# A four-layer conditional residual block: the transpose of the normalised rows moved from TensorE to VectorE

## The reference, cut to what matters

```
x = x + L0(x)    # adapter: relu(x @ W1 + b1) @ W2 + b2, plus x, layer norm over the row, * gamma + beta
x = x + L1(x)    # x @ weight[subject].T + bias
x = x + L2(x)    # two experts and three shared networks, relu(x @ wi) @ wo, mixed by a gate
x = x + L3(x)    # scores by tanh(x @ W1 + b1) @ v, masked softmax over rows, pooled rows
```

## Time and profile before

| | |
|---|---|
| median of 3 runs | 500.68 us (500.46 to 500.73) |
| the profiled execution | 501.22 us |
| its span, first to last instruction | 499.4 us |
| TensorE matmuls | 99% of the span busy |
| VectorE | 70% |
| ScalarE | 52% |
| GpSimd | 47% |

### The profile page before, as it was taken

How to read it: one execution, slowest core, us unless ns; L and a number is a source line. 1 busy time by engine, 2 the same in 40 slices (tenths; PEclk the granted TensorE clock), 3 DMA queues, 4 the chain that set the end, 5 groups by cost and what they waited for, 6 DMA issues and landing times.

```text
span 499.4 us, 6992 instructions
## 1 busy us (share of the span) xinstructions
PE 493.0 (99%) x2320; PEld 407.7 (82%) x2320; DVE 348.8 (70%) x702; ACT 260.3 (52%) x506; POOL 236.0 (47%) x201
## 2 busy tenths in 40 slices
PE   8999999999999999999999999999999999999996
PEld 5787888888888888888888888888888888888985
DVE  5587235885688799786478689788568779644467
ACT  4655555543457574444446656454345757445243
POOL 1575446445264446444544447444525444746023
PEclk9999999999999999999999999999999999999999
DMA  5865354322255443422227454422222342331002
GB/s 154 185 185 150 101 147 147 100 85 85 85 120 145 116 115 87 127 85 84 85 85 169 123 161 123 132 84 85 85 85 85 100 112 84 88 131 37 0 1 84
DMA packets 77657, 52.97 MB, mean 106 GB/s; under 512 B 40758, under 2 KB 67382, under 8 KB 77622
## 3 DMA queue, kind: packets, MB, share of 16 engines
q1 hardware_dynamic: 75734, 50.44, 35.5%
q10 hardware_dynamic: 1888, 2.10, 1.3%
HBM read 48.33 MB, written 2.10 MB: 101 GB/s over the span
## 4 chain that ended last, share of the span: by engine, by line
PE 90%; DVE 5%; DMA 3%; issue 1%; ACT 0%; ACTq 0%; DVEq 0%; SPq 0%
PE ps_hid L839 14%; PE ps_hid L840 14%; PE ps_hid L844 14%; PE ps_net L901 13%; PE ps_net L896 13%; PE ps_net L897 13%; DMA raw_wo<-in_L_cond_share_wo_dram 3%; PE ps_net L868 2%; DVE pick L1680 1%; DVE hid_lo L1827 1%; PE ps_side L537 1%; PE ps_side L541 1%; PE ps_side L536 1%; PE ps_side L547 1%; PE ps_side L550 1%
## 5 line engine op out<-in xcount | busy, mean ns | idle before, releaser
L1924 POOL TENSOR_TENSOR wi_lo<-raw_wi,wi_hi 128x512 fp32r<-128x512 f32 x77 | 101.6, 1319 | 207.5 <-ACT wo_hi L1088 110.2
L1109 ACT ACTIVATE hid_hi<-ps_hid 128x512 fp32r<-128x512 f32 x160 | 95.5, 598 | 194.1 <-PE ps_hid L844 192.3
L1827 DVE SCALAR_TENSOR_TENSOR hid_lo<-ps_hid,hid_hi 128x512 fp32r<-128x512 f32 x160 | 109.8, 688 | 113.9 <-ACT hid_hi L1109 112.5
L839 PE MATMUL ps_hid<-x2T_hi,wi_lo 128*128 128x512 f32 (+1 forms) x332 | 125.9, 381 | 0.0
L840 PE MATMUL ps_hid<-x2T_hi,wi_hi 128*128 128x512 f32 (+1 forms) x332 | 125.3, 379 | 0.0
L896 PE MATMUL ps_net<-hid_hi,wo_hi 128*128 128x512 f32 x304 | 118.9, 391 | 0.0
L897 PE MATMUL ps_net<-hid_hi,wo_lo 128*128 128x512 f32 x304 | 118.5, 390 | 0.0
L1925 POOL TENSOR_TENSOR wo_lo<-raw_wo,wo_hi 128x512 fp32r<-128x512 f32 x77 | 104.1, 1352 | 0.0
L844 PE MATMUL ps_hid<-x2T_lo,wi_hi 128*128 128x512 f32 (+1 forms) x332 | 98.9, 379 | 0.0
L901 PE MATMUL ps_net<-hid_lo,wo_hi 128*128 128x512 f32 x304 | 94.0, 390 | 0.3 <-DVE hid_lo L1827 0.3
L839 PEld LDWEIGHTS ps_hid<-x2T_hi,wi_lo 128*128 128x128 f32 x332 | 62.4, 188 | 11.9 <-POOL wo_lo L1925 0.2
(11 more groups left out here) (329 smaller groups left out, 500.1 us busy)
## 6 DMA issues: line engine op xcount, KB each, us to landing
raw_wi<-in_L_cond_share_wi_dram SPq DMA_DIRECT2D x23, 512.0 KB, 3.8
raw_wo<-in_L_cond_share_wo_dram SPq DMA_DIRECT2D x23, 512.0 KB, 4.8
raw_wi<-in_L_cond_expert_wi_dram SPq DMA_DIRECT2D x16, 512.0 KB, 3.8
raw_wo<-in_L_cond_expert_wo_dram SPq DMA_DIRECT2D x16, 512.0 KB, 4.8
next_x2T<-in_x_dram SPq DMA_DIRECT2D x24, 64.0 KB, 4.3
x_rows<-in_x_dram SPq DMA_DIRECT2D x3, 512.0 KB, 4.1
x_rows<-netT SPq DMA_DIRECT2D x48, 32.0 KB, 2.0
out_dram<-out_rows SPq DMA_DIRECT2D x5, 256.0 KB, 5.7
```

What stands on the lines that cost most here:

```text
L839: mm(dst, wi_lo[:, w, k, c], x2T_hi[:, k, rows], start=(k == 0), stop=False)
L1109: fn(hid_hi[:, ring(b, q)], ps_hid[:, ring(b, q)], ACT.Relu).then_inc(hid_hi_ready, 1)
L1827: v.scalar_tensor_tensor(out=hid_lo[:, ring(b, q)], in0=ps_hid[:, ring(b, q)], scalar=0.0, in1=f32(hid_hi[:, ring(b, q)]), op0=ALU.max, op ...
L1924: g.tensor_tensor(wi_lo[:, w], raw_wi[:, half % 2, :, c], f32(wi_hi[:, w]), ALU.subtract)
```

## The change

Three things change in `A_SLOT` and the code that reads it:

1. TensorE's transposes of `norm` are gone. VectorE does them in slots 30 and 31 with `turn_rows`: the four groups of 32 partitions of `norm` are read one after another, and each is transposed in blocks of 32 x 32 into each of the four groups of 32 partitions of `normT`, 16 instructions of 32 partitions x 256 elements. `normT` is `next_x2T`.
2. `w2`, `subj_blocks`, `hid`, `subj_w`, `adapt`, `stats` and `norm` each stand one slot earlier. `subj_wT` moves from `norm` to `next_x2T`, and TensorE's wait on `subj_w_lo` before the second half of the adapter product goes.
3. `xb` and both `x1` operations stand in slot 32; `x1` reads `normT` in SBUF in place of `ps_side` in PSUM. ScalarE rounds both halves of x1 in slot 34.

```diff
-    A_SLOT = dict(w1=20, blocks=20, xT=22, w2=25, subj_blocks=25, hid=26, subj_w=27, adapt=28, stats=29, xb=31, norm=30, normT=32, x1_hi=33, x1_lo=35, y=36, base=37)
+    A_SLOT = dict(w1=20, blocks=20, xT=22, w2=24, subj_blocks=24, hid=25, subj_w=26, adapt=27, stats=28, xb=32, norm=29, turn=30, x1=32, x1_hi=34, x1_lo=35, y=36, base=37)
...
-        subj_blocks, subj_wT = subj_w, norm[:, 0:KD]
+        subj_blocks, subj_wT = subj_w, next_x2T[:, :, 0:D]
+        normT = next_x2T
...
                             pe.wait_ge(a_dve.sem, a_dve.at(i, "hid_lo"))
-                        else:
-                            pe.wait_ge(a_dve.sem, a_dve.at(i, "subj_w_lo"))
                         adapt_half(ps_side[:, t], t).then_inc(a_pe.sem, 1)
...
-            def normalised(slot, i):
-                if 0 <= slot - A_SLOT["normT"] < KD:
-                    k = slot - A_SLOT["normT"]
-                    pe.wait_ge(a_dve.sem, a_dve.at(i, "norm"))
-                    for r in range(R):
-                        last = nc.tensor.transpose(ps_side[:, k, r * P:(r + 1) * P], norm[:, r, k * P:(k + 1) * P], ident[:])
-                    last.then_inc(a_pe.sem, 1)
...
-                if 0 <= slot - A_SLOT["x1_hi"] < KD:
-                    k = slot - A_SLOT["x1_hi"]
-                    act.wait_ge(a_dve.sem, a_dve.at(i, f"x1T{k}"))
-                    fn(opT_hi[:, k], x1T[:, k], ACT.Copy).then_inc(a_act.sem, 1)
+                if slot == A_SLOT["x1_hi"]:
+                    for k in range(KD):
+                        act.wait_ge(a_dve.sem, a_dve.at(i, f"x1T{k}"))
+                        fn(opT_hi[:, k], x1T[:, k], ACT.Copy).then_inc(a_act.sem, 1)
...
+                if slot == A_SLOT["x1"]:
+                    here("turn1")
+                    for k in range(KD):
+                        here(f"xb{k}")
+                        v.scalar_tensor_tensor(out=x1T[:, k], in0=normT[:, k], scalar=gamma[:, k:k + 1], in1=xbT[:, k],
+                                               op0=ALU.mult, op1=ALU.add).then_inc(a_dve.sem, 1)
...
+                if 0 <= slot - A_SLOT["turn"] < 2:
+                    h = slot - A_SLOT["turn"]
+                    here("norm")
+                    for a in (2 * h, 2 * h + 1):
+                        last = turn_rows(a)
+                    last.then_inc(a_dve.sem, 1)
...
+            def turn_rows(a):
+                for c in range(P // BK):
+                    rows = norm[a * BK:(a + 1) * BK].rearrange("p r (k d) -> p k r d", d=P)[:, :, :, c * BK:(c + 1) * BK]
+                    cols = normT[c * BK:(c + 1) * BK].rearrange("p k (r s) -> p k r s", s=P)[:, :, :, a * BK:(a + 1) * BK]
+                    last = v.transpose(cols, rows)
+                return last
```

More of the change, by code:

```diff
@@ L276, in cond_resid_program @@
         evac_dve = Steps(sem("evac_dve"), "g0 g1 g2 g3")
-        a_pe = Steps(sem("a_pe"), "hid adapt0 adapt1 normT0 normT1 y0 y1", 1)
+        a_pe = Steps(sem("a_pe"), "hid adapt0 adapt1 y0 y1", 1)
         a_act = Steps(sem("a_act"), "xhi0 xhi1 hid_below hid_up subj_w_hi x1hi0 x1hi1", 1)
         a_dve = Steps(sem("a_dve"), "w1_hi xT0 xT1 xlo0 xlo1 w2_hi w2_up b2_hi b2_lo subj_wT hid_sum hid_hi hid_lo subj_w_lo sum0 sum1 stats sums mean var_eps "
-                                    "norm xb0 xb1 x1T0 x1T1 x1lo0 x1lo1 x2T0 x2T1", 1)
+                                    "norm turn0 turn1 xb0 xb1 x1T0 x1T1 x1lo0 x1lo1 x2T0 x2T1", 1)
         a_pool = Steps(sem("a_pool"), "w1_lo w2_lo rstd", 1)
@@ L914, in batch @@
                         second_product(b, s, first, last)
-                    if not last:
-                        normalised(q, b + 1)
                     if not first:
```

## The result

The changed kernel takes 497.69 us (median of 6 runs, 497.30 to 498.81), against 500.73 us before in the same session (500.46 to 501.35): ratio 0.9942 (0.9929 to 0.9956), 3.0 us faster. The forecast was 498.0 us, in a range of 497.4 to 500.2. The profiled execution took 497.3 us, with a span of 495.5 us against 499.4.

The account below looks back on a forecast made before the run. TensorE, busy 493.0 of 499.4 us (99%), was taken to bound the kernel. Transposes removed (-3.00 us) and waiting for hT_both (+0.30) gave -2.7 us, from 500.68 to 498.0 us, range 497.4 to 500.2.

Parts of the forecast that it names:

- The bound, and the 3.00 us: TensorE, 99% busy, bounds the kernel; removing its 24 transposes saves 1.00 us a passage, 3.00 us for three.
- A wait less (subj_w_lo) costs nothing, and gives nothing where PE is busy throughout.: Adapter product on TensorE: dropping its wait on subj_w_lo was to change the time by nothing.
- The +0.30 for `hT_both`: Adapter product in slot 27: TensorE waits for ScalarE's hT_both 0.1 us a passage, 0.3 us in all.
- rival C: Half a gain: small delays (ScalarE's hT_both, x1_lo) sum to 0.5 us more a passage, 499.5 us; chance 0.08.
- The step of the block transposes, 0.45 us: VectorE, slots 30 and 31: 16 block transposes a passage start 0.45 us apart, 3.6 us in each slot.
- Rival B: Changing partition groups costs VectorE's transposes more: 502.7 us at a step of 0.575, 508.7 at 0.70; chance 0.10.
- The normalisations, 1.4 us: VectorE's four normalisations take 1.4 us, since GpSimd is idle until ScalarE has rounded slot 30's weights.
- Rival A: GpSimd slows VectorE: normalisations still take 3.32 us, 1.45 us waited a passage, 502.4 us; chance 0.12.
- From hid_lo to the end of var_eps take 2.90 us.: VectorE's chain from slot 28: hid_lo starts at 333.71, so var_eps is there at 336.6.
- The slack of 0.45: Smallest slack of VectorE's chain: x1_lo done at 354.85, its y product's load in slot 36 due at 355.30.
- Each further microsecond there, beyond 0.45, is a microsecond of TensorE in each passage.: VectorE's gapless chain from the normalisations to x1_lo: lateness beyond 0.45 us makes TensorE wait equally long.
- The sum: Whole kernel: -3.00 + 0.30 = -2.7 us, the median of the runs going from 500.68 to 498.0 us.

Follow-up runs that it names:

- e8: Changed kernel with the transposes back on TensorE, behind slots 31 and 32, and x1 read from PSUM in slot 33: 501.10 us, ratio 0.9997 to the kernel before.
- e2: Kernel before without TensorE's wait on subj_w_lo in the adapter product: 501.03 us, ratio 0.9993.
- e4: Changed kernel with the two loops of the block transposes exchanged, so four in a row write one partition group: 497.60 us, ratio 0.9928 to the kernel before.
- e7: Changed kernel with the four normalisations one slot later, in slot 30 beside GpSimd's weight split: 509.55 us, ratio 1.0170 to the kernel before.
- e9: Changed kernel with one more VectorE block transpose a passage, into a buffer nobody reads: 501.93 us, ratio 1.0015 to the kernel before.
- e11: Changed kernel with one more block transpose a passage, and the transposes written to PSUM, where x1 reads them: 500.39 us, ratio 0.9986 to the kernel before.
- e12: Changed kernel with two more block transposes a passage, and the transposes written to PSUM, where x1 reads them: 504.81 us, ratio 1.0066 to the kernel before.
- e5: Changed kernel with two more VectorE block transposes a passage, into a buffer nobody reads: 502.83 us, ratio 1.0032 to the kernel before.
- e6: Changed kernel with eight more VectorE block transposes a passage, into a buffer nobody reads: 509.21 us, ratio 1.0160 to the kernel before.
- e10: Changed kernel with the block transposes written to PSUM and x1 reading them there: 498.90 us, ratio 0.9954 to the kernel before.

## Why the prediction was right, point by point

- **The bound, and the 3.00 us.** Right to the hundredth: slots of 9.16 us became 8.16, and e8 gives the 1.00 us back with all else in the new order.
- **"A wait less (subj_w_lo) costs nothing, and gives nothing where PE is busy throughout."** Wrong: it gave 0.10 to 0.13 us a passage, 0.36 in all (e2). "Busy throughout" had been read from slots 32 to 34, not from the adapter's slot, and this wait of a tenth of a microsecond left no idle time in any row, only a matmul of 0.39 us in place of 0.28.
- **The +0.30 for `hT_both`.** Too careful: TensorE did not wait. In the trace after, ScalarE's copy ends at 325.24 + 0.62 = 325.86 and the first load that could want it stands at 325.94. The forecast had it at the end of a chain with one allowance (0.6 where 0.51 was the rule), ending between 0.1 us early and 0.1 late, and took the late end; it was 0.08 early. With that, nothing is left of rival C.
- **The step of the block transposes, 0.45 us.** Right (3.57 us for eight; 422 to 444 ns each). The reason was only half: changes of the input's group hold as well (e4). Rival B falls.
- **The normalisations, 1.4 us.** Right: 1.39. Rival A did not come about, though its mechanism is real (e7) and its price too low.
- **"From hid_lo to the end of var_eps take 2.90 us."** This is the step that failed. The value was taken from the earlier trace rows, where GpSimd was idle; one slot earlier the statistics lie beside the split, whose end the same paragraph had computed for `rstd`. They took 1.3 us longer. The forecast already let `rstd` wait 0.74 of that for the split, so that 0.65 reached the normalisations; of these 0.44 were left at the end of x1_lo, since x1_lo itself took 1.28 us, not 1.44. The slack of 0.45 became nil. That nothing showed of it in the time is luck: the slack was just enough, and the forecast had no reason for that. It was also less sure than it looked: with the durations as the prediction names them (0.61, 0.87, twice 0.75, 0.69) hid_lo(33) ends at 351.9, not 351.7, and the smallest slack is 0.2. The 0.45 takes overlaps of about 0.07 us at each step that it does not state, though the trace has them (x1 starts at 347.35, 0.79 us after an xb of 0.87). The same happened in slot 24, where two small operations took 1.30 and 1.40 us beside the split; nobody waited there.
- **"Each further microsecond there, beyond 0.45, is a microsecond of TensorE in each passage."** Wrong twice: it begins at 0, and one added transpose of 0.36 us cost 1.30 (e9), since lateness pushes x1 or xb into the next split. With x1 out of the lock it is one for one (e11), until xb reaches the split (e12).
- **The sum.** -2.7 us forecast. In the passages it was -3.35: -3.00 as forecast, -0.35 for the missed wait, 0 for the +0.30. The median of the runs moved by 3.04. Both of these misses left the forecast too slow, and they are small beside the 3.00 us; the third, in `var_eps`, was met by the slack.

Open: why e5, e6 and e9 stay 0.04 to 0.3 us under the sum of their parts (a room before the next wait would do that, but e10 shows none), and what makes slot 8 of batch 0 vary between 2.8 and 3.3 us. Neither was tried.

## What to carry to other kernels

When one engine is busy to 99%, handing its work to another can pay even at seven times the engine time (here 7.2 us of VectorE for 1.0 us of TensorE a passage), as long as the last reader still finds its data; so follow the receiving engine's chain to every place where the busy one reads from it. Take no duration along when an instruction moves to another time: look what GpSimd and VectorE do side by side there, and which of VectorE's operations read two SBUF tensors or, like `norm` and xb here, work from SBUF to SBUF with one. Slack that comes out at a few tenths of a microsecond should be tested with one added dummy operation, which shows at once whether the next delay costs its own length or a multiple.

## What the runs showed of the hardware that I had not expected

- VectorE and GpSimd exclude each other by whole instructions, and the size of the operation is no protection: one of four elements a partition took 1.26 us. Beside a split, `norm` (four operations) went from 1.39 to 3.33 us, two xb from 0.87 to 2.71, two x1 from 1.41 to 2.45, and GpSimd's own split from 1.29 to 1.74. Unaffected: transposes from SBUF to SBUF (eight in 3.59 us at 342.33, beside splits from 342.73 to 345.27), the first operation of the statistics (1.39 us beside the split and without), `hid_lo` and x1 with one operand in PSUM. The trace before had a second case that the prediction passed over: `hT_hi`, 1.41 us beside splits, is 0.42 after, where GpSimd is idle.
- After waiting 2.04 us for hid_lo in the third passage of e6 TensorE came back at the lower of its two clock levels: from 358.57 to 361.94 the granted clock was 0.51 of full speed, that is 1.2 GHz, and matmuls of 0.39 us took up to 0.63. The first passage, with a wait of 2.07 us, went the same way. The second had a wait of 2.05 us behind the same work, and the clock stayed at 1.00; its sum was 0.3 us shorter. So such a wait can cost the clock and need not; what decides it, e6 does not show. Timelines and stretches of e6, third passage and then second:

```profile
358.00 0.73 PE L892 MATMUL ps_net<-hid_lo,wo_hi 128*128 128x512 f32 x2 [2.04 <-DVE hid_lo L1834]
...
237.03 0.74 PE L892 MATMUL ps_net<-hid_lo,wo_hi 128*128 128x512 f32 x2 [2.05 <-DVE hid_lo L1834]
```
```profile
358.57:361.94 3.37, 3.37 (x9) 2.59 (x8) 3.37 (x5) 1.38 (x3) 0.98 (x1) 0.51 0.23 70
237.61:241.41 3.80, 3.04 (x14) 2.17 (x12) 3.80 (x6) 1.75 (x3) 0.97 (x1) 1.00 0.33 109
```
